# Nine-step places for a ternary quantiser inside an attention loop, its last four tiles moved to the next stage

## Chip, cores and metric

One core of a Trainium2 chip runs the whole program. The metric is device microseconds of one launch, the median of three runs. The engines are TensorE (PE, its weight loads PEld), VectorE (DVE), ScalarE (ACT), GpSimd (POOL) and the queues of DMAs issued by SyncE (SP) and ScalarE. Each takes its own instructions in order and waits on semaphores.

## What is computed

A transformer block with adaptive layer norm, B = 2, S = 1024, E = 512, 32 query heads on 8 key/value heads of 64:

```python
h = _layernorm(x) * (1 + ca) + sa
x = x + ga * attention(h, Wq, Wk, Wv, Wo)       # RoPE, causal softmax, grouped heads
h = _layernorm(x) * (1 + cb) + sb
gu = h @ ternary_quant(w_gate_up).T             # (4096, 512)
gate, up = split(gu)
hn = rms_norm(silu(gate) * up)
x = x + gb * (hn @ ternary_quant(w_proj).T)     # (512, 2048)

def ternary_quant(w, g=64):                     # in bf16, per group of 64
    scale = clip(mean(abs(w_g)), 1e-8)
    q = clip(round(w_g / scale), -1, 1)
    return w + (q * scale - w)
```

The float32 products are made of a high and a low part each (`_hi`, `_lo`), three matmuls instead of one.

## The kernel before

Four stages follow each other: a prologue (layer norm, first weights), attention, the output projection (`project_outputs`), the feed-forward network.

**Attention** runs over the 8 key/value heads g (bodies; a part of a body with g = -1 stands ahead of them and 12 steps behind them). A body is 72 steps T, written out by hand in one function `step(body, T)` per engine. Each step turns one 128 x 512 tile of exponentials (`turn`, PE L771), which ScalarE casts to `p_hi` (`high`, L855) and VectorE completes with `p_lo` (`low`, L963); two steps later TensorE multiplies it with the values (`values`, L785). So each `p_hi` and each `p_lo` marks a step. Score rows come with a period of nine steps: eight rows in nine steps, at 0, 1, 3, 4, 5, 6, 6, 7 (`ROW_AT`). A step later VectorE takes a row's maximum (`maximum`, L971, `negm`) and ScalarE its exponential (`exponentials`, L870, `p`). Score rows use four PSUM banks, so a row on TensorE waits for the exponential of two to four rows before (`ROW_FREED`). One PSUM bank collects value products; at the end of a block ScalarE copies it to `o_sb` (`copy_out`, L863), and the next block's first product waits for that.

Between these lie, at fixed steps: the projections of the next queries, keys and values on TensorE (`X_USES`), their rotation (`rotary_products`, L988 and L989, on VectorE; `rot_c`, `rot_x` on GpSimd), key casts `k_hh` (L939) and query casts `rot_s` (L943) on ScalarE, the scaling of `o_sb` on GpSimd, and the split of the next head's projection weights into high (ScalarE, T = 28) and low part (VectorE, T = 29, L1071), which TensorE's projection at T = 31 waits for.

The **quantiser** makes `ternary_quant` of one sixth of a 1/8 of the feed-forward weights at a time, six units u of 128 x 512 per body, one every 12 steps (`UNIT_STEPS`). Relative to 12u: load `wf` at 0, `w_abs` and `w_sign` on ScalarE at 3 (L947, L948), group sums `gsum` on VectorE at 4 (L1050), `gscale` at 5 (L1054), the threshold `above` at 6 (L1057), the pick (L1061) at 7, four GpSimd instructions at 8 to 11 (L1111 to L1121), store at 15 (ScalarE's queue). Units 0 to 3 are gate/up tiles, 4 and 5 down tiles; the results go to HBM. There is one place for `w_abs` and `w_sign`, so a unit's absolute values wait for the end of the unit before.

Within a step ScalarE runs, among others: `p_hi`, `o_sb`, exponentials, key and query casts, then the quantiser. VectorE: rotation, maxima, `p_lo`, then quantiser, weights' low part.

In the last body (g = 7) there is no next head to project from T = 28 on; instead the output weights and the first pieces of the attention output are split (`weights_high`, `weights_low`, `piece_high`, `piece_low`).

**The output projection** works on 4 chunks of 8 pieces; a piece is 24 matmuls and takes TensorE about 6 us. ScalarE and VectorE split the pieces of `o_raw` (L1211, L1215) with two pieces of lead. Beside it ScalarE loads stored ternary tiles (`load_tern`), TensorE turns them and ScalarE copies them for the feed-forward stage (`copy_turned`, L1328).

Of the kernel before, what the change touches and what calls it, by code (L numbers as in the profile page):

```python
# [202 lines left out]
def prologue(nc, ps, x, c, wmod, ident_in, ident, modT, hT_hi, hT_lo, vectors, late, load_first, load_tables, w_in, w_raw,  # L203
             rot, w_hi, w_lo, k_scaled, whi_ready, w_ready):
    with ExitStack() as ctx:  # L205
# [72 lines left out]
        def _(dve):  # L278
# [13 lines left out]
            dve.tensor_tensor(w_lo[:], w_raw[:], w_hi[:].bitcast(F32), ALU.subtract).then_inc(w_ready, 1)  # L292
# [48 lines left out]
UNITS, UNIT_STEPS = 6, 12  # L341
# [45 lines left out]
def attention_tensors(nc, ctx):  # L387
# [13 lines left out]
    rd_turned = sb("rd_turned", [P, 2, DEN_COLS], F32)  # L401
    wf = sb("wf", [P, UW], F32)
    w_abs = sb("w_abs", [P, UW], BF16)
    w_sign = sb("w_sign", [P, UW], BF16)
# [7 lines left out]
def attention(nc, ps, wq, wk, wv, w_gu, w_p, consts_in, w_in, w_raw, cos, sin, mask, ident, hT_hi, hT_lo, ot_dram, rden_dram,  # L412
              tern_gu, tern_p, o_sb, o_out,
              w_hi, w_lo, p_32, k_scaled, whi_ready, w_ready, vectors, late, modT, gates_dram, wmod, spare,
              tensors, rot, ident_b, tern_out, outputs):
    with ExitStack() as ctx:
# [188 lines left out]
        def _(sp):  # L605
# [42 lines left out]
            def step(body, T):  # L648
# [38 lines left out]
                if T == W_LOAD and body.holds(0, 0, KVH - 2):  # L687
                    sp.wait_ge(w_ready, body.g + 1)
# [8 lines left out]
        def _(pe):  # L697
# [139 lines left out]
        def _(act):  # L837
# [13 lines left out]

            def high(g, T):
# [29 lines left out]
            def step(body, T):  # L882
# [61 lines left out]
                for g, u in body.units(T, 3):  # L944
                    units_in.await_(act, g, u)
                    units_tern.await_(act, g, u - 1)
                    act.activation(w_abs[:], wf[:], ACT.Abs).then_inc(abs_ready, 1)  # L947
                    act.activation(w_sign[:], wf[:], ACT.Sign).then_inc(sign_ready, 1)  # L948
                for g, u in body.units(T, 15):
                    store_unit(g, u)  # L950
                for g, u in body.units(T, 0):
                    units_sign.await_(act, g, u - 1)
                    act.dma_start(unit_tile(u, wf), unit_of(g, u, gu_g, wp_g)).then_inc(wf_in, 16)

            bodies(act, step)
            outputs.scalar(act)
# [3 lines left out]
        def _(dve):  # L960
# [46 lines left out]

            def late_low(n, k):
# [4 lines left out]
            def step(body, T):  # L1013
# [34 lines left out]
                for g, u in body.units(T, 4):  # L1048
                    units_abs.await_(dve, g, u)
                    dve.tensor_reduce(gsum[:], w_abs[:].rearrange("p (g e) -> p g e", e=QG), AX.X,  # L1050
                                      ALU.add).then_inc(gsum_ready, 1)
                for g, u in body.units(T, 5):
                    units_sum.await_(dve, g, u)
                    dve.tensor_scalar(gscale[:], gsum[:], 1.0 / QG, 1e-8, ALU.mult, ALU.max).then_inc(gscale_ready, 1)  # L1054
                for g, u in body.units(T, 6):
                    units_scale.await_(dve, g, u)
                    dve.tensor_scalar(above[:], gscale[:], ROUND_HALF, None, ALU.mult).then_inc(above_ready, 1)  # L1057
                for g, u in body.units(T, 7):
                    units_above.await_(dve, g, u)
# [106 lines left out]
def project_outputs(nc, ctx, x, wo, tern_gu, tern_p, ot_dram, gates_dram, x2_dram, ident_b, wo_hi, wo_lo, places, wo_raw, wo_in, o_out,  # L1166
# [109 lines left out]
    def scalar(act):  # L1276
# [12 lines left out]
        def body(n, first):  # L1289
            if first:  # L1290
                act.wait_ge(terns_stored, 16 * UNITS * (KVH - 1))
# [550 lines left out]
```

## Time and profile before

| | |
|---|---|
| runs, median (lowest to highest) | 1844.34 us (1838.40 to 1846.98) |
| profiled execution | 1842.74 us, span 1840.8 us |
| mean granted TensorE clock | 0.992 |
| busy over the span: PE, PEld | 1745.0 us (95%), 1392.4 us (76%) |
| busy: DVE, ACT, POOL | 1260.5 (68%), 1146.8 (62%), 971.4 us (53%) |
| waits, longest in total: DVE `p_lo` for ACT `p_hi` | 187.5 us, 288 times |
| ACT `p` for DVE `negm` | 117.8 us, 153 times |
| PE scores L759 for ACT `p` | 41.6 us, 42 times |
| PE values L785 for ACT `o_sb` | 18.0 us, 31 times |

The profile is of one execution. Busy time of an engine is a share of the whole span; the stages differ, and a wait of an engine that isn't the bound costs nothing. A duration in the timeline includes time in which an instruction has been started and is held up.

### The profile page before, as it was taken

To read this page: it belongs to the slowest core of one execution; us is meant where nothing else is said; L and a number is where in the kernel's file an instruction comes from. 1 tells how busy PE (TensorE), PEld (TensorE's weight loads), DVE (VectorE), ACT (ScalarE), POOL (GpSimd) and SP (SyncE) were. 2 spreads that over 40 slices of the span, in tenths; PEclk is the share of its full clock that TensorE was granted. 3 is DMA by queue.
4 is the path that set the end of the run, shared out by engine and by line. 5 is a ranking of instruction groups with operands and counts; after the bars stand their busy time and mean duration, and the time that the engine had idled before them with its cause. 6 is when DMAs were issued, how large, how long until landed. Compare 5 with 4: busy or idle time off the path is not lost. (4 is left out here: it accounts for less than half of the span.)

```text
span 1840.8 us, 28072 instructions
## 1 busy us (share of the span) xinstructions
PE 1745.0 (95%) x9505; PEld 1392.4 (76%) x9505; DVE 1260.5 (68%) x2078; ACT 1146.8 (62%) x2315; POOL 971.4 (53%) x773
## 2 busy tenths in 40 slices
PE   7899999999999999999999999988999899999998
PEld 3587787777777777778777777866888788888886
DVE  6788888788788778788778878786333454535343
ACT  4677777777777777878777777785223353323221
POOL 1266657666667676666766666656000044444453
PEclk9999999999999999999999999999999999999999
DMA  7343444344344344344434435445555300101000
GB/s 277 88 111 84 123 106 117 102 111 127 81 127 117 85 127 113 89 118 107 124 101 108 120 89 138 110 138 170 190 183 178 130 1 1 52 1 52 1 29 23
DMA packets 174969, 190.95 MB, mean 104 GB/s; under 512 B 31456, under 2 KB 117736, under 8 KB 174832
## 3 DMA queue, kind: packets, MB, share of 16 engines
q1 hardware_dynamic: 137840, 140.99, 26.9%
q10 hardware_dynamic: 36992, 48.25, 9.4%
q8 instruction: 72, 1.18, 0.3%
q14 instruction: 65, 0.53, 0.1%
HBM read 86.12 MB, written 31.74 MB: 64 GB/s over the span
## 5 line engine op out<-in xcount | busy, mean ns | idle before, releaser
L963 DVE TENSOR_TENSOR p_lo<-ps_b,p_hi 128x512 fp32r<-128x512 f32 x576 | 395.6, 687 | 191.4 <-ACT p_hi L855 187.5
L870 ACT ACTIVATE p<-ps_b,negm 128x640 f32<-128x640 f32 (+7 forms) x512 | 382.0, 749 | 120.7 <-DVE negm L971 117.8
L855 ACT CAST p_hi<-ps_b 128x512 fp32r<-128x512 f32 x576 | 337.2, 588 | 152.8 <-PE ps_b L771 150.1
L971 DVE TENSOR_REDUCE negm<-ps_b 128x1 f32<-128x640 f32 (+7 forms) x512 | 376.1, 745 | 35.4 <-PE ps_b L761 34.7
L771 PE MATMUL ps_b<-ident,p 128*128 128x128 f32 x2304 | 351.0, 275 | 7.7 <-DVE p_lo L963 6.8
L759 PE MATMUL ps_b<-k_hh,q_hl 128*128 128x512 f32 (+3 forms) x768 | 271.2, 353 | 42.7 <-ACT p L870 41.6
L785 PE MATMUL ps_b<-p_hi,v_hl 128*128 128x512 f32 x576 | 277.2, 481 | 18.3 <-ACT o_sb L863 18.0
L771 PEld LDWEIGHTS ps_b<-ident,p 128*128 128x128 f32 x2304 | 259.1, 141 | 42.8 <-DVE p_lo L963 8.9
L760 PE MATMUL ps_b<-k_l,q_hl 128*128 128x512 f32 (+3 forms) x768 | 257.3, 348 | 0.0
L786 PE MATMUL ps_b<-p_lo,v_hl 128*128 128x512 f32 x576 | 227.9, 396 | 0.0
L759 PEld LDWEIGHTS ps_b<-k_hh,q_hl 128*128 128x128 f32 x768 | 146.0, 190 | 91.8 <-ACT p L870 60.9
L1550 PE MATMUL ps_d<-h_hi,gu 128*128 128x512 f32 x512 | 200.5, 392 | 1.9 <-DVE h_lo L1670 1.9
L1551 PE MATMUL ps_d<-h_lo,gu 128*128 128x512 f32 x512 | 199.9, 390 | 0.0
L1086 POOL TENSOR_TENSOR o_sb<-o_sb,o_low 64x512 f32<-64x512 f32 x128 | 178.5, 1399 | 37.5 <-DMA o_low<-o_sb 37.4
L1095 POOL TENSOR_TENSOR rot_c<-rot_c,rot_x 128x512 f32<-128x512 f32 (+1 forms) x96 | 126.8, 1321 | 101.6 <-DMA rot_x<-rot_s 100.8
L1106 POOL TENSOR_TENSOR rot_x<-rot_c,rot_s 128x512 fp32r<-128x512 f32 x64 | 82.2, 1284 | 165.0 <-ACT rot_s L943 165.0
L760 PEld LDWEIGHTS ps_b<-k_l,q_hl 128*128 128x128 f32 x768 | 145.7, 190 | 27.9
L1091 POOL TENSOR_TENSOR o_sb<-o_sb,rd_all 64x512 f32<-64x512 f32 x128 | 164.0, 1286 | 3.9
L723 PE MATMUL ps_b<-hT_hi,w_hi 128*128 128x512 f32 x384 | 159.3, 415 | 2.2 <-PEq L205 1.3
L1646 POOL TENSOR_TENSOR sq<-a 128x512 f32<-128x512 f32 x60 | 71.1, 1185 | 163.9 <-DVE a L1720 163.4
L724 PE MATMUL ps_b<-hT_hi,w_lo 128*128 128x512 f32 x384 | 150.8, 393 | 0.0
L725 PE MATMUL ps_b<-hT_lo,w_hi 128*128 128x512 f32 x384 | 150.3, 391 | 0.0
(159 smaller groups left out, 3202.8 us busy)
## 6 DMA issues: line engine op xcount, KB each, us to landing
rot_x<-rot_s SPq DMA_DIRECT2D x320, 64.0 KB, 2.0
q_hl<-rot_s SPq DMA_DIRECT2D x128, 128.0 KB, 2.5
q_hl<-rot_x SPq DMA_DIRECT2D x128, 128.0 KB, 2.5
rd_all<-reciprocals SPq DMA_DIRECT2D x128, 128.0 KB, 3.1
o_low<-o_sb ACTq DMA_DIRECT2D x128, 128.0 KB, 2.4
attention_out<-o_sb SPq DMA_DIRECT2D x128, 128.0 KB, 2.5
o_raw<-attention_out SPq DMA_DIRECT2D x32, 512.0 KB, 4.5
wf<-in_L_ffn_w_gate_up ACTq DMA_DIRECT2D x32, 256.0 KB, 2.9
```

The costliest lines, as they stand in the source:

```text
L759: pe.matmul(ps[:, bank, 0:n], q, k_hh[unit][:, k0:k0 + n], start=True, stop=False)
L760: ins = pe.matmul(ps[:, bank, 0:n], q, k_l0[:, unit, k0:k0 + n], start=False, stop=(k0 + n < nk))
L771: ins = pe.transpose(ps[:, T_BANK + T % 2, h * P:(h + 1) * P], p_32[:, parity, h, column * P:(column + 1) * P], ident[:])
L785: pe.matmul(ps[:, O_BANK, :], v_hl[unit][:, j, :], p_hi[:, T % P_RING, :], start=(j == 0), stop=False)
L786: pe.matmul(ps[:, O_BANK, :], v_hl[unit][:, j, :], p_lo[:, T % P_RING, :], start=False, stop=(j == i)).then_inc(pv_done, 1)
L855: act.copy(p_hi[:, T % P_RING, :], ps[:, T_BANK + T % 2, :]).then_inc(phi_ready, 1)
L870: act.activation(p_32[:, parity, h, column * P:column * P + nk], s, ACT.Exp, bias=negm[:, k:k + 1], scale=1.0, accum_out=den[:, parity, k: ...
L963: dve.tensor_tensor(p_lo[:, T % P_RING, :], ps[:, T_BANK + T % 2, :], p_hi[:, T % P_RING, :].bitcast(F32), ALU.subtract).then_inc(plo_read ...
L971: dve.tensor_reduce(negm[:, k:k + 1], s, AX.X, ALU.max, negate=True).then_inc(max_ready, 1)
L1086: pool.tensor_tensor(o_sb[0:D, n % 2, :], o_sb[0:D, n % 2, :], o_low[:, n % 2, :], ALU.add).then_inc(o_added, 1)
L1550: pe.matmul(ps[:, bank + half, :], gu[:, m, half, k, :], h_hi[:, parity, k, :], start=(k == 0), stop=False)
L1551: i = pe.matmul(ps[:, bank + half, :], gu[:, m, half, k, :], h_lo[:, parity, k, :], start=False, stop=(k == CT - 1))
```

## The change

1. The quantiser's steps go to tables with a period of nine: abs and signs at T = 8, 17, ... 53 (`UNIT_ABS`), sum, scale and threshold together at 11, 20, ... 56 (`UNIT_SUM`), pick at 17, 26, ... 62 (`UNIT_PICK`), GpSimd's parts one to four steps and the store six steps after the pick. Loads stand one step after the abs of the unit before.
2. `w_abs` and `w_sign` get two places; abs of unit u waits for the end of unit u - 2.
3. The low part of the projection weights is made in four quarters, at T = 29 to 32, and each k of the projection waits for its quarter. The prologue does it in quarters too.
4. Down tiles become units 0 and 1, gate/up tiles 2 to 5. Units 2 to 5 of the last body leave the loop: they run in the first chunk of the output projection at pieces 0, 2, 4, 6 (`LATE_UNIT_AT`), loaded into a buffer of their own (`wf_late`). The load of the last ternary tiles waits for their stores in the second chunk only.

```diff
-            dve.tensor_tensor(w_lo[:], w_raw[:], w_hi[:].bitcast(F32), ALU.subtract).then_inc(w_ready, 1)
+            for k in range(CT):
+                dve.tensor_tensor(w_lo[:, k], w_raw[:, k], w_hi[:, k].bitcast(F32), ALU.subtract).then_inc(w_ready, 1)
...
-UNITS, UNIT_STEPS = 6, 12
+UNITS = 6
+UNIT_ABS, UNIT_SUM, UNIT_PICK = (8, 17, 26, 35, 44, 53), (11, 20, 29, 38, 47, 56), (17, 26, 35, 44, 53, 62)
+UNIT_LOAD = (0,) + tuple(at + 1 for at in UNIT_ABS[:-1])
+UNIT_STORE = tuple(at + 6 for at in UNIT_PICK)
+UNIT_POOL = [tuple(at + part for at in UNIT_PICK) for part in range(1, 5)]
+LAST_UNITS = 2
...
-    w_abs = sb("w_abs", [P, UW], BF16)
-    w_sign = sb("w_sign", [P, UW], BF16)
+    w_abs = sb("w_abs", [P, 2, UW], BF16)
+    w_sign = sb("w_sign", [P, 2, UW], BF16)
...
+                        if table[u] - STEPS * back == T and self.holds(back, 0, KVH - 1 if u < LAST_UNITS else KVH - 2)]
...
-                if k == 0:
-                    if n == X_HERE:
-                        splits_lo.await_(pe, g, 0)
+                if n == X_HERE:
+                    splits_lo.await_(pe, g, k)
+                if k == 0:
...
+            def unit_raw(g, u):
+                return places.wf_late if g == KVH - 1 and u >= LAST_UNITS else wf
+            def unit_load(g, u):
+                units_sign.await_(act, g, u - 1)
+                act.dma_start(unit_tile(u, unit_raw(g, u)), unit_of(g, u, gu_g, wp_g)).then_inc(wf_in, 16)
+            def unit_parts(g, u):
+                units_in.await_(act, g, u)
+                units_tern.await_(act, g, u - 2)
+                act.activation(w_abs[:, u % 2], unit_raw(g, u)[:], ACT.Abs).then_inc(abs_ready, 1)
+                act.activation(w_sign[:, u % 2], unit_raw(g, u)[:], ACT.Sign).then_inc(sign_ready, 1)
...
-                for g, u in body.units(T, 3):
+                for g, u in body.units(T, UNIT_ABS):
+                    unit_parts(g, u)
+                for g, u in body.units(T, UNIT_STORE):
                     store_unit(g, u)
+                for g, u in body.units(T, UNIT_LOAD):
+                    unit_load(g, u)
...
+                for g, u in body.units(T, UNIT_SUM):
+                    unit_sum(g, u)
+                    unit_scale(g, u)
+                    unit_above(g, u)
+                for g, u in body.units(T, UNIT_PICK):
+                    unit_pick(g, u)
...
-                if body.split(T, W_LOW):
-                    splits_hi.await_(dve, body.g, 0)
-                    dve.tensor_tensor(w_lo[:], w_raw[:], w_hi[:].bitcast(F32), ALU.subtract).then_inc(w_ready, 1)
+                for k in range(CT):
+                    if body.split(T, W_LOW + k):
+                        splits_hi.await_(dve, body.g, 0)
+                        dve.tensor_tensor(w_lo[:, k], w_raw[:, k], w_hi[:, k].bitcast(F32), ALU.subtract).then_inc(w_ready, 1)
...
+                for part in range(4):
+                    for g, u in body.units(T, UNIT_POOL[part]):
+                        UNIT_PARTS[part](g, u)
...
+                if first and s in LATE_UNIT_AT:
+                    u = LAST_UNITS + LATE_UNIT_AT.index(s)
+                    if u > LAST_UNITS:
+                        unit_store(KVH - 1, u - 1)
+                    unit_parts(KVH - 1, u)
+                    if u + 1 < UNITS:
+                        unit_load(KVH - 1, u + 1)
...
+                if first and s in LATE_UNIT_AT:
+                    unit_scales(KVH - 1, LAST_UNITS + LATE_UNIT_AT.index(s))
...
         pool.memset(free[:], 0.0).then_inc(x2_out[1], 16)
+        for u in range(LAST_UNITS, UNITS):
+            unit_rounded(KVH - 1, u)
```

## Rows read from the trace of the kernel before

**Rows 1.** Windows: start:end, length, then busy us (instructions) per engine, PEclk, DMA share, GB/s.
```profile
531.67:681.76 150.09, 143.53 (x849) 115.30 (x848) 121.30 (x204) 115.90 (x252) 99.36 (x81) 1.00 0.42 110
1188.56:1275.50 86.94, 71.86 (x401) 54.61 (x400) 74.00 (x115) 67.67 (x139) 53.05 (x39) 0.94 0.47 139
1275.50:1333.00 57.50, 57.50 (x288) 46.79 (x287) 15.75 (x13) 15.72 (x16) 5.78 (x6) 1.00 0.65 203
```
**Rows 2.** Waits of PE in 531.67 to 681.76 us: total us, times, longest.
```profile
PE ps_b L759 <- ACT p L870: 4.2, 5, 1.3
PE ps_b L785 <- ACT o_sb L863: 2.1, 4, 0.7
```
**Rows 3.** Groups by form, attention stage: busy us, mean ns of one, idle before.
```profile
L1061 DVE TENSOR_TENSOR w_hat<-w_abs,above 128x512 bf16<-128x512 bf16 x48 | 40.8, 850 | 0.0
...
L1057 DVE TENSOR_SCALAR above<-gscale 128x8 f32<-128x8 bf16 x48 | 18.1, 378 | 0.0
```
**Rows 4.** Timeline of ACT, steps 8 and 9, and 44: start us, us, instruction, [idle before].
```profile
550.70 0.47 ACT L870 ACTIVATE p<-ps_b,negm 128x256 f32<-128x256 f32 x1 [0.60 <-DVE negm L971]
...
551.63 0.60 ACT L863 COPY o_sb<-ps_b 128x512 f32<-128x512 f32 x1
...
625.82 0.48 ACT L870 ACTIVATE p<-ps_b,negm 128x256 f32<-128x256 f32 x1 [0.37 <-DVE negm L971]
```
**Rows 5.** Timeline of DVE, a chain of dependent small instructions before the feed-forward stage.
```profile
1460.62 0.16 DVE L83 TENSOR_TENSOR tmp_d<-rstd_d 128x4 f32<-128x4 f32 x1
1460.82 0.16 DVE L84 TENSOR_TENSOR tmp_d<-tmp_d,var_d 128x4 f32<-128x4 f32 x1
```
**Rows 6.** Timeline of DVE and POOL, in the last body and in the feed-forward stage.
```profile
1196.92 1.28 POOL L1086 TENSOR_TENSOR o_sb<-o_sb,o_low 64x512 f32<-64x512 f32 x1
1197.03 1.20 DVE L1057 TENSOR_SCALAR above<-gscale 128x8 f32<-128x8 bf16 x1
...
1612.68 1.35 POOL L1648 TENSOR_TENSOR ssq<-ssq,sq 128x512 f32<-128x512 f32 x1
1612.92 1.67 DVE L1670 TENSOR_TENSOR h_lo<-h_d,h_hi 128x512 fp32r<-128x512 f32 x1
```
**Rows 7.** Timeline of DVE, step 12.
```profile
557.24 0.69 DVE L963 TENSOR_TENSOR p_lo<-ps_b,p_hi 128x512 fp32r<-128x512 f32 x1 [0.68 <-ACT p_hi L855]
```
**Rows 8.** Timeline of DVE, steps 28 to 31.
```profile
592.37 0.64 DVE L1050 TENSOR_REDUCE gsum<-w_abs 128x8 f32<-128x512 bf16 x1
...
594.66 0.40 DVE L1054 TENSOR_SCALAR gscale<-gsum 128x8 bf16<-128x8 f32 x1
594.97 1.75 DVE L1071 TENSOR_TENSOR w_lo<-w_raw,w_hi 128x1536 fp32r<-128x1536 f32 x1
596.64 0.68 DVE L963 TENSOR_TENSOR p_lo<-ps_b,p_hi 128x512 fp32r<-128x512 f32 x1
597.24 0.66 DVE L1057 TENSOR_SCALAR above<-gscale 128x8 f32<-128x8 bf16 x1
597.81 1.21 DVE L971 TENSOR_REDUCE negm<-ps_b 128x1 f32<-128x1024 f32 x1
```
**Rows 9.** Timeline of ACT and DVE, steps 39 and 40.
```profile
615.62 0.63 ACT L947 ACTIVATE w_abs<-wf 128x512 bf16<-128x512 f32 x1
...
616.28 1.07 DVE L971 TENSOR_REDUCE negm<-ps_b 128x1 f32<-128x896 f32 x1
616.80 0.58 ACT L911 COPY rot_c<-ps_b 64x512 f32<-64x512 f32 x1
...
617.89 1.01 ACT L870 ACTIVATE p<-ps_b,negm 128x896 f32<-128x896 f32 x1
```
**Rows 10.** Timeline of DVE, step 55 of the second and of the fourth body.
```profile
348.71 0.65 DVE L1061 TENSOR_TENSOR w_hat<-w_abs,above 128x512 bf16<-128x512 bf16 x1
...
648.84 1.76 DVE L1061 TENSOR_TENSOR w_hat<-w_abs,above 128x512 bf16<-128x512 bf16 x1
```
**Rows 11.** Timeline of DVE, step 67 of the last body.
```profile
1269.97 1.36 DVE L1061 TENSOR_TENSOR w_hat<-w_abs,above 128x512 bf16<-128x512 bf16 x1
```
**Rows 12.** Timeline of ACT, first piece of the output projection.
```profile
1281.27 1.05 ACT L1211 CAST o_hi<-o_raw 128x1024 fp32r<-128x1024 f32 x1 [4.96 <-PE ps_c L1260]
```

More of the change, by code:

```diff
@@ L1006, in gate_step, with unit_sum, unit_scale, unit_above @@
                                              op1=ALU.mult).then_inc(vectors.gates_done, 1)
+            def unit_sum(g, u):
+                units_abs.await_(dve, g, u)
+                dve.tensor_reduce(gsum[:], w_abs[:, u % 2].rearrange("p (g e) -> p g e", e=QG), AX.X, ALU.add).then_inc(gsum_ready, 1)
+            def unit_scale(g, u):
+                units_sum.await_(dve, g, u)
+                units_hat.await_(dve, g, u - 1)
+                dve.tensor_scalar(gscale[:], gsum[:], 1.0 / QG, 1e-8, ALU.mult, ALU.max).then_inc(gscale_ready, 1)
+            def unit_above(g, u):
+                units_scale.await_(dve, g, u)
+                dve.tensor_scalar(above[:], gscale[:], ROUND_HALF, None, ALU.mult).then_inc(above_ready, 1)
+            def unit_pick(g, u):
+                units_above.await_(dve, g, u)
+                units_out.await_(dve, g, u - 1)
+                dve.tensor_tensor(w_hat[:].rearrange("p (g e) -> p g e", e=QG), w_abs[:, u % 2].rearrange("p (g e) -> p g e", e=QG),
+                                  above[:].unsqueeze(2).broadcast_to([P, NG, QG]), ALU.is_gt).then_inc(picked, 1)
+            def unit_scales(g, u):
+                for part in (unit_sum, unit_scale, unit_above, unit_pick):
+                    part(g, u)
             def late_low(n, k):
@@ L1047, in step @@
                     dve.transpose(rd_turned[:, n % 2, :], rd[:, n % 2, :]).then_inc(rd_flipped, 1)
[L1048 to L1059, printed above, removed]
-                    units_out.await_(dve, g, u - 1)
-                    dve.tensor_tensor(w_hat[:].rearrange("p (g e) -> p g e", e=QG), w_abs[:].rearrange("p (g e) -> p g e", e=QG),
-                                      above[:].unsqueeze(2).broadcast_to([P, NG, QG]), ALU.is_gt).then_inc(picked, 1)
+                for g, u in body.units(T, UNIT_SUM):
[4 more added lines that the diff above has]
+                    unit_pick(g, u)
                 for i in range(8):
@@ L1138 @@
 TURN_LAG, COPY_LAG = 1, 2
+LATE_UNIT_AT = (0, 2, 4, 6)
 TERNS, GU_TERNS = 6, 4
@@ L1296, in body @@
                     piece_high(act, n, s, first)
+                if first and s in LATE_UNIT_AT:
[5 more added lines that the diff above has]
+                        unit_load(KVH - 1, u + 1)
+                if first and s == NPC - 1:
+                    unit_store(KVH - 1, UNITS - 1)
                 if s - COPY_LAG in TERN_AT:
@@ L1300, in body @@
                     if first and u + 2 == GU_TERNS:
+                        act.wait_ge(terns_stored, 16 * (UNITS * (KVH - 1) + LAST_UNITS))
+                    if not first and u + 2 == GU_TERNS // 2:
                         act.wait_ge(terns_stored, 16 * UNITS * KVH)
```

76 lines of the change are left out of this document (37 added, 39 removed).

## Prediction

> **What bounds the kernel now.** I read the stage windows first [rows 1]. In one steady body of the attention loop (531.67 to 681.76 us, 150.09 us for 72 steps) TensorE's matmuls are busy 143.53 us at the full granted clock, the 2.4 GHz level. So TensorE sets the time and at most 6.6 us of a body, some 46 us over seven bodies, can be won. VectorE (121.3), ScalarE (115.9) and GpSimd (99.4) all have room on average, so what counts is where their queues are late. In the stretch 1188.56 to 1275.50, the last 44 steps of the eighth body, TensorE is busy only 71.86 of 86.94 us at clock 0.94: there the other two engines set the pace. In the output projection after it TensorE is never idle. The wait view says what TensorE waits for in the body [rows 2]: score rows wait for an exponential to free a bank (4.2 us, five times), value products for the copy of `o_sb` (2.1 us, four times). Both run on ScalarE, and the exponential itself stands behind VectorE's `negm`. Each is a short in-order chain of a few steps, and the quantiser's instructions are in some of them. Steps below are T of a body; each `p_hi` cast marks one.
>
> **What one unit costs.** The change keeps every instruction of the quantiser and moves it. ScalarE pays 1.18 us from `w_abs` to the instruction behind the signs (615.62 to 616.80) [rows 9]. VectorE pays 0.6 us for `gsum`, and for `gscale`, `above` and the pick 0.07 to 0.1, 0.07 to 0.1 and 0.6 us when nothing stands in the way. They are dearer as they are: `above` averages 378 ns and the pick 850 [rows 3]. New is that sum, scale and threshold stand in one step, each waiting for the one before. Dependent small instructions follow each other every 0.20 us [rows 5], so the group costs 0.65 + 0.2 + 0.2, about 1.05 us, if GpSimd is quiet.
>
> It often isn't. `above`, eight columns wide, took 1.20 us from 1197.03, to 1198.23; GpSimd's `o_sb` had run from 1196.92 to 1198.20. And an `h_lo` that follows its own producer took 1.67 us, not 0.69, from 1612.92, because GpSimd's next instruction (1612.68) had got in between [rows 6]. So such an instruction waits for a whole GpSimd instruction of about 1.25 us, and two dependent ones can each wait. GpSimd is busy 66% of a body. A group should meet a wait of 0.66 x 0.63 = 0.4 us for the first and, if another GpSimd instruction is ready in 4 of 10 cases, 0.4 x 1.25 = 0.5 us for the second: 0.9 us on top, with ends 0 and 2.4. Worse, GpSimd's four parts now run at T=18 to 21, 27 to 30, 36 to 39, 45 to 48, 54 to 57, just where the groups of the next units stand (20, 29, 38, 47, 56).
>
> The Trainium skill says the same of the pair of ports (SBUF — State Buffer, "SBUF: two separate sides"): it is an exclusive lock that a VectorE instruction with two SBUF inputs, or in a 2-port mode, and a GpSimd instruction hold in turn, the loser blocked in full. By that rule the quarters of `w_lo` can be held up too, which the row of 1.75 us doesn't show. On the other hand the skill's VectorE: DVE Perf Modes, "The DRAIN you can't avoid", has a semaphore between chained VectorE instructions cost nothing; by it a group would be 0.8 and not 1.05 us, and the four groups of a body that matter below would cost 1.0 us less a body: 1857 us. The 0.20 us cadence speaks against it.
>
> **Place by place, per body.**
> (a) Abs and sign at T=8, ahead of `p_hi` and `o_sb` of T=9, for which TensorE's first value product waits already. ScalarE was idle for 0.60 us there, behind VectorE [rows 4], which loses scale, threshold and pick of T=5 to 7 and so ends that wait: +1.18 - 0.60 = +0.55 (0 to 1.2).
> (b) The same at T=44, behind two `k_hh` casts. The idle time before that exponential is 0.37 [rows 4], and about 0.3 comes from the sum that leaves T=40: +0.5 (0 to 1.2).
> (c) The group at T=11. VectorE had 0.68 us idle before the `p_lo` that leads to the maximum that TensorE waits for in T=14 [rows 7]. 1.05 + 0.9 - 0.68: +1.2 (0.3 to 2.5).
> (d) T=26 to 34, the worst stall now. The chain on VectorE loses `gsum` 0.56, `gscale` 0.31, the whole `w_lo` 1.67 and `above` 0.57, together 3.1 us [rows 8]. It gets the group (1.05 + 0.9) and two quarters before the maximum of T=31 (each 0.42 + 0.05, and 0.5 of blocking for both): 3.4. +0.3; the third quarter for the pick, and abs and sign one step earlier ahead of the same `w_hi`: about +0.1. +0.4 (-1.2 to 2.6).
> (e) T=39. Abs and sign leave ScalarE (-1.18), but the exponential at 617.89 can't then start before VectorE's `negm` ends at 617.35 [rows 9], and the group at T=38 adds 1.05 + 0.9 less 0.98 idle: +0.4 (-0.5 to 0.9).
> (f) T=53 to 59. The pick leaves T=55, where it took 1.76 us in five bodies of seven and 0.65 in the others, which don't stall there [rows 10]: -0.5 on average; the group at T=56 comes in: +1.0. +0.5 (-0.4 to 1.2).
> (g) Groups at T=20 and 47, in steps with more room: +0.4 (0 to 1.3). At T=62 the pick takes the place of the sum of T=64: 0.
> Sum +3.95 a body, +27.7 for seven. The eighth body has (a), (c) and half of (g): +1.9.
>
> **The four late tiles.** From T=27 of the eighth body ScalarE's four pairs (4.7 us) and VectorE's chains go; one pick alone took 1.36 us [rows 11]. On the path I count 2.3 us at T=28 to 32 (sum, blocked threshold, pick), 1.3 at 39 to 43, 1.6 at 51 to 55, 2.4 at 64 to 67, and 1.4 of GpSimd no longer blocking the weights' low parts: -9 (-5 to -12). TensorE's 15 idle us there are the ceiling; a granted clock that stays up is in it. In the output projection the same work meets ScalarE idle for 4.96 us [rows 12] and more than 5 us on VectorE per piece of 6 us. The new wait is ScalarE's for the store of the tile before, behind GpSimd's 4.6 us; queued behind it are the next `copy_turned` and `o_hi`, with about 0.7 us to spare at the third piece: +0.5 (0 to 4). Its cover is TensorE's own 6 us a piece. Prologue quarters, the second place for signs and the swapped order of tiles: 0.
>
> 27.7 + 1.9 - 9 + 0.5 = +21.1 on the profiled execution's 1842.74 us (span 1840.8), which is 1.6 below the median of the runs: **1863.8 us**.
>
> **Rivals.** (1) The gaps hold the work: GpSimd is never in the way. Then (a) and (b) 0.55 + 0.5, (c) 0.3, (d) -1.15, (e) -0.5, (f) -0.35, (g) 0: -0.65 a body, -4.6; with +0.9 in the eighth and -9: 1830 us, the other side. Its place is the group: it decides when the wait of `gscale` and `above` stays under about 0.25 us together. For it: no score row needs a maximum in steps 3, 12, 21. Against: 66% GpSimd. 0.24. (2) Gains and losses cancel: the groups are blocked but half as long, +1 a body; 7 + 1.5 - 9 + 0.5: 1843. 0.17. (3) Every group meets two full GpSimd instructions, by the skill's rule of the lock too, where GpSimd has always work ready: +7.8 a body (0.5, 0.5, 1.6, 3.3, 0.8, 1.1), 55 + 2.6 - 8 + 1: 1893. 0.14; my forecast in its own bounds 0.45.
>
> **How the numbers follow.** A measurement of this kernel tells about 0.5% (9 us) from no change. Range 1827 to 1893: from rival 1 with the last body at its -12 to rival 3. Faster 0.24 (rival 1), same 0.17 (rival 2), slower 0.59 (forecast and rival 3).
>
> **What would show it.** In the body, TensorE's wait for `o_sb` should grow at T=10 and 46 (about 0.5 us each), its wait for exponentials in T=14, 41 and 59; `above` should average over 0.6 us, the body should be 153 to 155 us long. The stretch from T=27 of the last body should fall from 86.9 to about 78 us; the output projection should stay gapless. A body of 149 us with `above` at 0.16 us would prove the forecast wrong at its main step, a longer projection at its last.

## The result and the profile after

The changed kernel took 1913.73 us (median of four runs, 1911.48 to 1919.24); beside it the kernel before took 1842.55 (1838.40 to 1846.98). The ratio is 1.0396 (95% interval 1.0381 to 1.0411): 4% slower. I had forecast 1863.8 and a range of 1827 to 1893. The direction was right, the size was not.

The page of the changed kernel, for the rows that stand in the table of before (groups: busy us, mean ns | idle time before them, and what ended most of it):

```profile
span 1909.6 us, 28143 instructions
...
PE 1771.0 (93%) x9505; PEld 1407.7 (74%) x9505; DVE 1325.5 (69%) x2102; ACT 1144.1 (60%) x2315; POOL 961.5 (50%) x773
...
L778 PE MATMUL ps_b<-ident,p 128*128 128x128 f32 x2304 | 355.2, 277 | 14.2 <-DVE p_lo L979 14.1
L766 PE MATMUL ps_b<-k_hh,q_hl 128*128 128x512 f32 (+3 forms) x768 | 273.1, 356 | 52.3 <-ACT p L890 49.8
L792 PE MATMUL ps_b<-p_hi,v_hl 128*128 128x512 f32 x576 | 280.0, 486 | 17.8 <-ACT o_sb L883 17.3
L730 PE MATMUL ps_b<-hT_hi,w_hi 128*128 128x512 f32 x384 | 165.0, 430 | 25.4 <-DVE w_lo L1102 17.9
```

And of the kernel before, for `p_lo`:

```profile
L771 PE MATMUL ps_b<-ident,p 128*128 128x128 f32 x2304 | 351.0, 275 | 7.7 <-DVE p_lo L963 6.8
```

TensorE's wait for exponentials grew from 41.6 to 49.8 us and the one for `o_sb` shrank by 0.7. What grew most is TensorE behind VectorE: from 6.8 to 14.1 us for `p_lo`, and 17.9 us for the quarters of `w_lo`, where no such wait stood before. VectorE is 65 us busier, although it has the same work: a busy VectorE instruction can be one that is held up.

**Where the 68.8 us of span went.** Windows of the kernel after (the first row is the sum of its seven full bodies, from 84.74 to 1205.17 us; then the fourth body, a stretch in it, the eighth body to its step 27 and from there on, and the output projection's first 58 us):

```profile
sum 1120.43, PE 1029.69 PEld 821.87 DVE 914.69 ACT 809.16 POOL 679.05; mean PE 147.10 PEld 117.41 DVE 130.67 ACT 115.59 POOL 97.01
...
565.57:726.41 160.84, 148.29 (x850) 118.19 (x849) 130.85 (x207) 115.47 (x252) 97.85 (x81) 0.97 0.39 103
635.80:639.00 3.20, 3.20 (x11) 2.57 (x10) 3.20 (x5) 0.87 (x1) 2.21 (x2) 0.50 0.14 48
1205.17:1262.03 56.86, 54.86 (x329) 44.67 (x328) 45.38 (x77) 42.84 (x94) 30.74 (x25) 1.00 0.40 111
1262.03:1339.40 77.37, 67.81 (x402) 51.31 (x401) 65.20 (x100) 63.34 (x131) 37.73 (x27) 0.98 0.49 141
1339.40:1397.00 57.60, 52.84 (x264) 42.31 (x263) 23.12 (x28) 19.16 (x23) 28.87 (x21) 1.00 0.66 204
```

and the sum of the seven full bodies before:

```profile
sum 1050.82, PE 1003.49 PEld 806.06 DVE 848.76 ACT 811.71 POOL 690.95; mean PE 143.36 PEld 115.15 DVE 121.25 ACT 115.96 POOL 98.71
```

The seven bodies are 69.6 us longer. TensorE's idle time in them went from 47.3 to 90.7 us (+43.4), and its busy time for the same matmuls from 1003.5 to 1029.7 (+26.2). The second part is the clock: in the fourth body the granted clock is 0.97 and not 1.00 as before [rows 1], and from 635.80 to 639.00 it is 0.50, the 1.2 GHz level. The last stretch of the eighth body fell from 86.94 us [rows 1] to 77.37, while its first 27 steps grew from 55.64 to 56.86; all of that body went from 142.6 to 134.2. Behind it everything is 4.9 us longer. Ahead of the first body it is 2.6: there TensorE is busy 66.08 us at a granted clock of 0.90, before 63.80 us at 0.96, for the same 253 matmuls. 69.6 - 8.4 + 4.9 + 2.6 = 68.7, which is the 68.8 but for rounding.

**One body, wait by wait.** TensorE's idle times in the fourth body after (timeline of PE, [idle before <- what ended it]; not shown are seven with 3.61 us together, which were there before or are small):

```profile
586.55 0.50 PE L792 MATMUL ps_b<-p_hi,v_hl 128*128 128x512 f32 x1 [0.36 <-ACT o_sb L883]
596.55 0.44 PE L766 MATMUL ps_b<-k_hh,q_hl 128*128 128x384 f32 x1 [1.26 <-ACT p L890]
...
635.45 0.58 PE L730 MATMUL ps_b<-hT_hi,w_hi 128*128 128x512 f32 x1 [2.52 <-DVE w_lo L1102]
...
666.91 0.50 PE L792 MATMUL ps_b<-p_hi,v_hl 128*128 128x512 f32 x1 [0.74 <-ACT o_sb L883]
674.92 0.50 PE L730 MATMUL ps_b<-hT_hi,w_hi 128*128 128x512 f32 x1 [0.87 <-DVE rot_s L1005]
...
695.70 0.66 PE L778 MATMUL ps_b<-ident,p 128*128 128x128 f32 x4 [1.33 <-DVE p_lo L979]
698.54 0.80 PE L766 MATMUL ps_b<-k_hh,q_hl 128*128 128x512 f32 x1 [1.72 <-ACT p L890]
```

They stand in T = 10, 14, 31, 46, 49, 58 and 59. Before, three others stood in T = 32, 41 and 59:

```profile
600.32 0.33 PE L759 MATMUL ps_b<-k_hh,q_hl 128*128 128x128 f32 x1 [0.97 <-ACT p L870]
...
619.04 0.38 PE L759 MATMUL ps_b<-k_hh,q_hl 128*128 128x256 f32 x1 [0.56 <-ACT p L870]
...
656.37 0.50 PE L759 MATMUL ps_b<-k_hh,q_hl 128*128 128x512 f32 x1 [0.60 <-ACT p L870]
```

**What stands behind T = 31 and 58.** Timeline of DVE, steps 29 and 56, and then of POOL at both places:

```profile
631.60 2.32 DVE L1035 TENSOR_SCALAR above<-gscale 128x8 f32<-128x8 bf16 x1
633.83 1.57 DVE L1102 TENSOR_TENSOR w_lo<-w_raw,w_hi 128x384 fp32r<-128x384 f32 x1
...
691.50 3.55 DVE L1035 TENSOR_SCALAR above<-gscale 128x8 f32<-128x8 bf16 x1
694.97 0.68 DVE L979 TENSOR_TENSOR p_lo<-ps_b,p_hi 128x512 fp32r<-128x512 f32 x1
```

```profile
631.50 1.16 POOL L1125 TENSOR_TENSOR w_hat<-w_abs,w_hat 128x512 bf16<-128x512 bf16 x1
632.62 1.25 POOL L1146 TENSOR_TENSOR rot_c<-rot_c,rot_x 128x512 f32<-128x512 f32 x1
...
691.39 1.16 POOL L1125 TENSOR_TENSOR w_hat<-w_abs,w_hat 128x512 bf16<-128x512 bf16 x1
692.52 1.28 POOL L1142 TENSOR_TENSOR o_sb<-o_sb,rd_all 64x512 f32<-64x512 f32 x1
693.76 1.26 POOL L1157 TENSOR_TENSOR rot_x<-rot_c,rot_s 128x512 fp32r<-128x512 f32 x1
```

`above`, 8 columns wide, was started at 691.50, 0.11 us behind a GpSimd instruction, and ended at 695.05, when `rot_x` ended: three GpSimd instructions, two of which began after it. At 631.60 it was two. The `p_lo` and the first quarter of `w_lo` stand behind it in VectorE's queue, and TensorE behind these. The same comes back in every body: `above` takes 3.55 to 3.57 us at each T = 56, and 2.3 us at T = 29 in five of seven bodies (3.42 in one; in the last of the seven the scale takes 2.42 instead). That gave my theory A: such instructions are held up by a whole run of GpSimd's, and nearly all of the loss hangs on it. The rivals: the quarters of `w_lo` do it (B), the chaining of small dependent instructions (C), or the placement of the other parts (on ScalarE, and the two places).

### The profile page after: what moved, and what is told of

Read it like the earlier page. It is cut to its first block and busy times, and to the rows that moved or that the text cites. A ratio compares the mean times of both kernels' runs of the same rounds, so it can differ in the third digit from the quotient of the medians.

```text
span 1909.6 us, 28143 instructions
## 1 busy us (share of the span) xinstructions
PE 1771.0 (93%) x9505; PEld 1407.7 (74%) x9505; DVE 1325.5 (69%) x2102; ACT 1144.1 (60%) x2315; POOL 961.5 (50%) x773
## 5 line engine op out<-in xcount | busy, mean ns | idle before, releaser
L778 PE MATMUL ps_b<-ident,p 128*128 128x128 f32 x2304 | 355.2, 277 | 14.2 <-DVE p_lo L979 14.1
L766 PE MATMUL ps_b<-k_hh,q_hl 128*128 128x512 f32 (+3 forms) x768 | 273.1, 356 | 52.3 <-ACT p L890 49.8
L1137 POOL TENSOR_TENSOR o_sb<-o_sb,o_low 64x512 f32<-64x512 f32 x128 | 168.2, 1315 | 104.1 <-DMA o_low<-o_sb 104.1
L730 PE MATMUL ps_b<-hT_hi,w_hi 128*128 128x512 f32 x384 | 165.0, 430 | 25.4 <-DVE w_lo L1102 17.9
L731 PE MATMUL ps_b<-hT_hi,w_lo 128*128 128x512 f32 x384 | 156.4, 407 | 0.0
L732 PE MATMUL ps_b<-hT_lo,w_hi 128*128 128x512 f32 x384 | 155.3, 405 | 0.0
```

Source lines behind the costliest of these rows:

```text
L766: pe.matmul(ps[:, bank, 0:n], q, k_hh[unit][:, k0:k0 + n], start=True, stop=False)
L778: ins = pe.transpose(ps[:, T_BANK + T % 2, h * P:(h + 1) * P], p_32[:, parity, h, column * P:(column + 1) * P], ident[:])
L1137: pool.tensor_tensor(o_sb[0:D, n % 2, :], o_sb[0:D, n % 2, :], o_low[:, n % 2, :], ALU.add).then_inc(o_added, 1)
```

## The experiments

All ratios are against the kernel before on the same chip.

| kernel | us | ratio, 95% interval |
|---|---|---|
| e1 old places, late tiles | 1841.43 | 1.0000 (0.9990 to 1.0011) |
| e2 whole low part | 1912.15 | 1.0390 (1.0371 to 1.0408) |
| e3 group in three steps | 1879.94 | 1.0215 (1.0195 to 1.0235) |
| e4 summing form | 1849.55 | 1.0046 (1.0029 to 1.0063) |
| e5 old places, late tiles, summing | 1833.99 | 0.9962 (0.9946 to 0.9977) |
| e6 before, summing | 1830.85 | 0.9947 (0.9932 to 0.9962) |
| e7 GpSimd's parts apart | 1878.69 | 1.0198 (1.0179 to 1.0216) |
| e8 threshold fused into the pick | 1846.05 | 1.0025 (1.0012 to 1.0038) |
| e9 = e5, late tiles untied | 1825.32 | 0.9926 (0.9912 to 0.9939) |
| e10 = e6, threshold fused | 1830.72 | 0.9951 (0.9937 to 0.9964) |
| e11 = e4, whole low part | 1845.64 | 1.0033 (1.0020 to 1.0046) |
| e12 = e9, threshold fused | 1822.90 | 0.9912 (0.9899 to 0.9926) |

TensorE's idle time in the fourth body, in us (from the timelines of PE: at two places, and in all):

| kernel | T = 31, 32 | T = 58, 59 | whole body |
|---|---|---|---|
| before | 0.97 | 0.60 | 6.6 |
| after | 2.52 | 3.05 | 12.5 |
| e2 whole low part | 3.69 | 3.08 | 13.4 |
| e3 group in three steps | 1.97 | 2.70 | 11.3 |
| e7 GpSimd's parts apart | 3.75 | 0 | 11.0 |
| e4 summing form | 3.22 | 0 | 7.8 |
| e8 threshold fused | 3.19 | 0 | 7.5 |

### e1: the places undone

```diff
-UNIT_ABS, UNIT_SUM, UNIT_PICK = (8, 17, 26, 35, 44, 53), (11, 20, 29, 38, 47, 56), (17, 26, 35, 44, 53, 62)
+UNIT_ABS, UNIT_SUM, UNIT_SCALE, UNIT_ABOVE, UNIT_PICK, UNIT_STORE = [tuple(12 * u + at for u in range(6)) for at in (3, 4, 5, 6, 7, 15)]
+UNIT_LOAD = tuple(12 * u for u in range(6))
...
-                for k in range(CT):
-                    if body.split(T, W_LOW + k):
+                if body.split(T, W_LOW):
```

> The changed kernel with the quantiser's steps of the kernel before (period of twelve, sum, scale, threshold and pick in four steps) and the whole low part in one instruction; the four late tiles, the swapped order of tiles and the two places stay. Theory: all of the loss in the bodies comes from the places. Then a body is 150.1 us again, the stretch of the last body stays at about 78.7 us (-8.2) and the later stages keep their +5: 1839 us, ratio 0.998 (0.996 to 1.000). Rival: the second places or the order of tiles cost in the bodies by themselves; then a body stays over 152 us and the ratio is over 1.005.

The body is 150.05 us again, and the last body 132.5. Windows of e1 (fourth body, eighth body, first 57 us of the output projection), and what TensorE and VectorE wait for at the start of the output projection (us in total, times, longest):

```profile
532.10:682.15 150.05, 143.44 (x849) 115.28 (x848) 120.48 (x204) 115.84 (x252) 99.51 (x81) 1.00 0.42 110
1133.18:1265.70 132.52, 122.18 (x730) 95.94 (x729) 110.07 (x176) 106.37 (x225) 70.04 (x53) 0.99 0.47 130
1265.70:1323.00 57.30, 51.98 (x254) 41.39 (x253) 22.46 (x28) 19.16 (x23) 28.94 (x21) 0.97 0.65 202
```

```profile
PE ps_c L1305 <- DVE o_lo L1262: 5.3, 3, 3.1
...
DVE w_hat L1039 <- DMA ternary<-w_hat: 8.1, 2, 5.8
```

So the order of the tiles and the second places cost nothing in the bodies, and the rest of the change alone is the loss. The four late tiles gain 10 us in the last body (142.6 to 132.5) and give back 5.9 behind it (571.2 us to the end of the span, not 565.3). In the medians nothing of it is left.

### e2 and e11: the quarters undone, with and without what stands ahead of them

```diff
-                for k in range(CT):
-                    if body.split(T, W_LOW + k):
-                        splits_hi.await_(dve, body.g, 0)
-                        dve.tensor_tensor(w_lo[:, k], w_raw[:, k], w_hi[:, k].bitcast(F32), ALU.subtract).then_inc(w_ready, 1)
+                if body.split(T, W_LOW):
+                    splits_hi.await_(dve, body.g, 0)
+                    dve.tensor_tensor(w_lo[:], w_raw[:], w_hi[:].bitcast(F32), ALU.subtract).then_inc(w_ready, CT)
```

> The changed kernel, only the low part of the projection weights made in one instruction at T = 29 again. Theory A (the threshold in T = 29 stands 2.3 us behind GpSimd's instructions, and all that is queued behind it is late): the low part still starts 2.8 us late, so the wait of the projection in T = 31 stays at 2.5 to 3.5 us and the ratio at 1.035 to 1.040. Theory B (the quarters do it: each can be held up by itself, 1.57 and 1.04 us instead of 0.5): the wait in T = 31 falls under 1 us, the body loses 3 us or more, ratio 1.025 or less.

> e4 with the whole low part in one instruction at T = 29. In e2 the quarters could show nothing, because what stood ahead of them was 2.5 us late. Here nothing is: if quarters help at all (a projection that can start after the first), this kernel loses against e4 1 us a body, ratio 1.008 to 1.010; if a quarter that waits for GpSimd costs as much as it saves, it stays at 1.0046 +- 0.002.

e2 is the changed kernel within 0.1%, and its wait at T = 31 is longer and not shorter (3.69 us, where I had said 2.5 to 3.5): the quarters are not the cause, theory B falls. e11 takes away the threshold's wait first (as e4, below), and even then the whole is not worse than the quarters (1.0033 against 1.0046, the intervals overlap), where I expected 1.008 if quarters helped. The low parts in the summing kernels e4 and e11 (count: ns min/median/max):

```profile
L1104 DVE TENSOR_TENSOR w_lo<-w_raw,w_hi x28: 540/1080/2786, 144.7 to 1060.0; 128x384 fp32r<-128x384 f32 x28
```

```profile
L1103 DVE TENSOR_TENSOR w_lo<-w_raw,w_hi x7: 3648/3906/5022, 145.1 to 1049.0; 128x1536 fp32r<-128x1536 f32 x7
```

A quarter takes 0.54 us alone and up to 2.79 held up, the whole never less than 3.65 here, against 1.75 in the kernel before [rows 8]. Both are held up themselves in the new places. That the quarters lose by four chances of being held what they win by an early start fits this, but no run shows it by itself.

### e3: the group taken apart

```diff
+UNIT_SCALE, UNIT_ABOVE = tuple(at + 1 for at in UNIT_SUM), tuple(at + 2 for at in UNIT_SUM)
...
+                for g, u in body.units(T, UNIT_SCALE):
                     unit_scale(g, u)
+                for g, u in body.units(T, UNIT_ABOVE):
                     unit_above(g, u)
```

> The changed kernel with scale and threshold one and two steps behind the sum (T = 12, 21, 30 ... and 13, 22, 31 ...), the period of nine and all else as it is. Theory A (a wait for GpSimd's run of back-to-back instructions, placed in front of the first quarter and of a p_lo cast): the first quarter in T = 29 no longer stands behind the threshold, the wait in T = 31 falls by 2 us or more, that of T = 58 to 60 by 2 us or more, since GpSimd's run is broken up differently; ratio 1.015 to 1.028. Theory C (only the small dependent instructions cost, 0.2 us each): -0.4 us a group in the four groups that matter, ratio 1.033. Rival: scale and threshold are held up just as long in their new steps and hit the projection's quarters from there: ratio 1.035 or more.

### e7: GpSimd's parts moved away from the group

```diff
-UNIT_STORE = tuple(at + 6 for at in UNIT_PICK)
-UNIT_POOL = [tuple(at + part for at in UNIT_PICK) for part in range(1, 5)]
+UNIT_STORE = tuple(at + 7 for at in UNIT_PICK)
+UNIT_POOL = [tuple(at + part for at in UNIT_PICK) for part in (1, 2, 4, 5)]
```

> The changed kernel (plain scale and threshold) with GpSimd's four parts at one, two, four and five steps behind the pick and the store at seven, so that none stands in the step of the group (three steps behind a pick). Theory A1 (it is the coincidence of the quantiser's own parts with the groups): the threshold of T = 29 and 56 falls to one GpSimd instruction or less (under 1.3 us), the waits of T = 31 and 58 to 60 lose 4 us together, ratio 1.010 to 1.022. Theory A2 (GpSimd's other work is enough: the two o_sb instructions and a rotation make the same run): the two thresholds stay over 2 us and the ratio over 1.030.

Both win half of the loss back (1.0215 and 1.0198), inside what theory A and A1 asked, but not in the way they said: in e3 the wait at T = 31 falls from 2.52 to 0.18 us, but 1.8 us come in at T = 32, and at T = 58 and 59 only 0.3 goes; in e7 the second place loses its wait whole and the first has 1.2 us more. In both an instruction of the group is still held up. Here are `above` and `gscale` of the kernel after:

```profile
L1035 DVE TENSOR_SCALAR above<-gscale x48: 171/1146/3565, 111.1 to 1375.0; 128x8 f32<-128x8 bf16 x48
...
L1031 DVE TENSOR_SCALAR gscale<-gsum x48: 170/274/2420, 109.7 to 1374.8; 128x8 bf16<-128x8 f32 x48
```

and `gscale` of e3, in its step behind the sum:

```profile
L1032 DVE TENSOR_SCALAR gscale<-gsum x48: 161/671/3256, 108.1 to 1342.7; 128x8 bf16<-128x8 f32 x48
```

In e7 the two places part ways. The wait at T = 56 is gone, as A1 said; at T = 29 it grew, as A2 said, and fell on the scale (timeline of DVE):

```profile
617.05 2.63 DVE L1031 TENSOR_SCALAR gscale<-gsum 128x8 bf16<-128x8 f32 x1
619.72 1.19 DVE L1035 TENSOR_SCALAR above<-gscale 128x8 f32<-128x8 bf16 x1
620.82 1.58 DVE L1102 TENSOR_TENSOR w_lo<-w_raw,w_hi 128x384 fp32r<-128x384 f32 x1
...
678.59 0.17 DVE L1035 TENSOR_SCALAR above<-gscale 128x8 f32<-128x8 bf16 x1
```

The GpSimd instructions ahead of the first of these lines:

```profile
616.01 1.28 POOL L1142 TENSOR_TENSOR o_sb<-o_sb,rd_all 64x512 f32<-64x512 f32 x1
617.26 1.28 POOL L1146 TENSOR_TENSOR rot_c<-rot_c,rot_x 128x512 f32<-128x512 f32 x1
```

The scale came 0.24 us before the end of `o_sb` and waited for `rot_c` and a `w_hat` behind it as well. So neither the quantiser's own parts alone nor GpSimd's other work alone make the run. Theory C (0.2 us for each dependence) asked 1.033 of e3; it falls. (The trace of e7 is of its longest execution, 1888.73 us; the median is 1878.69.)

### e4: the instructions that can't be held up

```diff
-                dve.tensor_scalar(gscale[:], gsum[:], 1.0 / QG, 1e-8, ALU.mult, ALU.max).then_inc(gscale_ready, 1)
+                dve.tensor_scalar(gscale[:], gsum[:], 1.0 / QG, 1e-8, ALU.mult, ALU.max,
+                                  accum_out=unused[:, 0:1]).then_inc(gscale_ready, 1)
...
-                dve.tensor_scalar(above[:], gscale[:], ROUND_HALF, None, ALU.mult).then_inc(above_ready, 1)
+                dve.tensor_scalar(above[:], gscale[:], ROUND_HALF, 0.0, ALU.mult, ALU.max,
+                                  accum_out=unused[:, 1:2]).then_inc(above_ready, 1)
```

> The changed kernel with scale and threshold in the form that also sums its output into a spare word (accumulator output); same places, same values. It tells whether scale and threshold are held up as instructions that take the ports shared with GpSimd, which the summing form does not do by the Trainium skill's page SBUF - State Buffer. Theory A: the threshold of T = 56 falls from 3.55 to 0.2 us and that of T = 29 from 2.3 to 0.2, the waits of T = 31 and 58 to 60 fall by about 5 us together, the clock stays up; body 153 to 155 us, ratio 1.012 to 1.022. Rival: the duration is a wait for something else (a semaphore of GpSimd's scaling of the unit before) and stays: ratio 1.04.

The threshold of e4, all 48 of it, and the windows of its fourth body:

```profile
L1036 DVE TENSOR_SCALAR_CACHE_REDUCE above<-gscale x48: 160/161/164, 106.8 to 1310.4; 128x8 f32<-128x8 bf16 x48
```

```profile
533.80:685.10 151.30, 143.48 (x849) 115.15 (x848) 122.62 (x219) 115.58 (x252) 97.91 (x81) 1.00 0.42 109
```

From 171 to 3565 ns the threshold went to 160 to 164, at the same places, against the same GpSimd work; the ratio went from 1.0396 to 1.0046. By the medians some 63 of 71 us hang on the form of two instructions of eight columns. It beat even my figure for theory A (1.012 to 1.022; a body of 153 to 155 us). Of the body's 9.5 us, 4.7 are idle time, near the 5 that I expected: the wait at T = 58 and 59 is gone, that at T = 31 fell to 1.43, but 1.8 us of waits came in at T = 32. The other 4.8 are the clock, which I had named and not counted in full: it is 1.00 and TensorE's busy time 143.48 us, as before the change. The 26 us of slow matmuls were a consequence of the waits, not a loss of their own.

The Trainium skill states the rule by which I chose this experiment (SBUF — State Buffer, "Who interferes with whom"): `tensor_scalar` can take the port pair that VectorE shares with GpSimd, but not in the form that also writes its accumulator, and `tensor_tensor` with both inputs in SBUF contends too. The rows agree on each: `above` in its two forms, and the quarters of `w_lo`, which are held up in e4 still.

### e5 and e6: the same in the old places, with and without late tiles

e6 is the kernel before with e4's two edits (an accumulator output for `gscale` and for `above`), e5 is e1 with the same two.

> The old places with the late tiles (as e1) and, besides, scale and threshold in the summing form. Theory A (such an instruction is held up by GpSimd wherever it stands, in the old places by 0.3 to 1.1 us now and then): the threshold of T = 30 falls from 0.57 to 0.17 us and the body from 150.1 to 149.3 us, ratio 0.996. Rival: in the old places nothing on the path hangs on it, the ratio stays at 1.000 +- 0.001; or the second instruction of the summing form (0.08 us) costs and it is 1.002.

> The kernel before, with scale and threshold in the summing form only. Beside e5 it tells what the four late tiles bring by themselves: their last body is 9.8 us shorter and the stages behind it 5.9 us longer in e1. If that holds, this kernel is at 0.998 and e5 0.002 below it; if the late tiles bring nothing in the runs, both are the same.

The kernel before was paying too: e6 is 0.5% faster than it. Its fourth body:

```profile
526.00:675.20 149.20, 143.18 (x849) 115.22 (x848) 118.44 (x216) 116.10 (x252) 98.79 (x81) 1.00 0.41 110
```

Against e4's 151.30 that also says what the new places, quarters included, cost when nothing is held up in scale and threshold: 2.1 us in this body, 16.3 in the seven (1056.75 against 1040.45). The late tiles I had expected to bring e5 under e6; it is 3 us above, with overlapping intervals: as built they bring nothing.

### e8 and e10: no threshold instruction

```diff
-                dve.tensor_tensor(w_hat[:].rearrange("p (g e) -> p g e", e=QG), w_abs[:, u % 2].rearrange("p (g e) -> p g e", e=QG),
-                                  above[:].unsqueeze(2).broadcast_to([P, NG, QG]), ALU.is_gt).then_inc(picked, 1)
+                dve.scalar_tensor_tensor(out=w_hat[:].rearrange("p (g e) -> p g e", e=QG),
+                                         in0=gscale[:].unsqueeze(2).broadcast_to([P, NG, QG]), scalar=ROUND_HALF,
+                                         in1=w_abs[:, u % 2].rearrange("p (g e) -> p g e", e=QG),
+                                         op0=ALU.mult, op1=ALU.is_lt).then_inc(picked, 1)
...
-                    unit_above(g, u)
```

> The changed kernel without the threshold instruction: the pick multiplies the scale by the constant itself and compares, in one instruction (scalar_tensor_tensor), and gscale keeps its plain form. Theory A: gscale takes over the wait, since it is an instruction of the same kind that is ready 0.2 us earlier; only the second wait goes (0.2 + half of 2 us): the waits of T = 31 and 58 to 60 lose 1 to 3 us, ratio 1.015 to 1.030. Rival (only the threshold is affected, not the scale): as in e4, ratio 1.005.

> The kernel before without the threshold instruction (the pick multiplies and compares in one) and with the scale in the summing form. If the single threshold instruction and its 0.2 us behind the scale are on the path anywhere in the old places, this is 0.001 to 0.002 under e6 (0.9947); else the same as e6.

e8 refuted me: the plain scale did not take over the wait, and 1.0025 is as good as e4 (the intervals overlap). The timeline of DVE in its T = 29, and of POOL:

```profile
597.36 0.27 DVE L1031 TENSOR_SCALAR gscale<-gsum 128x8 bf16<-128x8 f32 x1
597.55 2.82 DVE L1103 TENSOR_TENSOR w_lo<-w_raw,w_hi 128x384 fp32r<-128x384 f32 x1
```

```profile
596.32 1.28 POOL L1143 TENSOR_TENSOR o_sb<-o_sb,rd_all 64x512 f32<-64x512 f32 x1
597.57 1.15 POOL L1126 TENSOR_TENSOR w_hat<-w_abs,w_hat 128x512 bf16<-128x512 bf16 x1
598.69 1.25 POOL L1147 TENSOR_TENSOR rot_c<-rot_c,rot_x 128x512 f32<-128x512 f32 x1
```

The scale was started 0.24 us before `o_sb` ended and got in at the boundary, ahead of `w_hat`. The quarter behind it came as this `w_hat` began, and waited for it and for `rot_c`, as the threshold did in the kernel after. In e7 the scale was just as early against the same `o_sb`, but `rot_c` was next, and it did not get in: how early it is does not decide by itself. e10 is e6 again (0.9951 and 0.9947): in the old places no one waits for the threshold once it can't be held.

### e9 and e12: late tiles that hold nobody up

```diff
-                    if u > LAST_UNITS:
-                        unit_store(KVH - 1, u - 1)
...
-                for part in (unit_sum, unit_scale, unit_above, unit_pick):
+                for part in (unit_sum, unit_scale, unit_above):
...
+                if first and s - 1 in LATE_UNIT_AT:
+                    unit_pick(KVH - 1, LAST_UNITS + LATE_UNIT_AT.index(s - 1))
...
+                pool.dma_start(to, unit_tile(u, w_hat)).then_inc(places.late_out, 16)
```

> As e5 (old places, summing form, late tiles), but in the output projection the pick stands one piece later, behind the low part of that piece, and GpSimd issues the stores of the four tiles itself, so neither VectorE's low parts nor ScalarE's high parts stand behind a store. Theory D: the three waits of TensorE for o_lo (5.3 us in e1) are all that the late tiles cost there; they go, and the kernel is 5 to 7 us under e5: ratio 0.993. Rival: the cost is GpSimd and VectorE holding each other up, or DMA traffic: ratio 0.996 as e5.

> e9 and e10 together: old places, no threshold instruction, summing scale, late tiles with their stores on GpSimd. If the gains add up: 0.991 to 0.993; if e10 brings nothing: as e9.

In e1 the pick of a late tile waited for the store of the tile before, and the copies on ScalarE stood behind a store that waited for GpSimd (timelines of DVE and of ACT in e1; the pick, and the copy behind the last store):

```profile
1307.83 0.69 DVE L1039 TENSOR_TENSOR w_hat<-w_abs,above 128x512 bf16<-128x512 bf16 x1 [5.82 <-DMA ternary<-w_hat]
```

```profile
1314.69 1.01 ACT L1387 COPY wp_b<-ps_t 128x1024 bf16<-128x1024 bf16 x1 [8.94 <-POOL w_hat L1130]
```

The store that this pick waited for was issued at 1299.80 us, as soon as GpSimd had ended, and took 7.9 us to land (the median of these stores is 2.4); four loads of `o_raw` were issued from 1296.61 on. In e9 the longest of the four late stores takes 4.6 us, the pick waits 2.6 us in all, with no low part behind it, and TensorE has no wait for `o_lo` in the output projection's first chunk:

```profile
1257.70:1315.00 57.30, 57.30 (x287) 46.67 (x286) 23.18 (x37) 20.12 (x24) 27.44 (x25) 1.00 0.70 227
```

e9 is 6.6 us under e5 by the ratios (0.9926 and 0.9962, their intervals just apart): theory D holds, though e9 doesn't part the moved pick from the moved stores. The late tiles are a gain of their own once untied: e12 with them is at 0.9912, e10 without them at 0.9951, and the intervals are apart (those of e9 and e6, 0.9926 and 0.9947, overlap). e12, with the threshold fused as well, is 2.4 us below e9, which its interval doesn't tell from it. At 0.9912 it is 16 us faster than the kernel before and 91 us faster than the change.

## Why the prediction was wrong

The fourth body after against the one before, TensorE's idle time by place:

| place | forecast | measured |
|---|---|---|
| (a) T = 10, `o_sb` | +0.55 | +0.36 |
| (b) T = 46 | +0.5 | +0.03 |
| (c) T = 14 | +1.2 | +1.26 |
| (d) T = 29 to 34 | +0.4 (to 2.6) | +1.3: 2.52 at T = 31, less 0.97 at T = 32 and 0.25 at T = 29 |
| (e) T = 41 | +0.4 | -0.56 |
| (f) T = 58, 59 | +0.5 (to 1.2) | +2.45 |
| (g) T = 23, 24, 49 | +0.4 (to 1.3) | +1.4 |
| T = 6 and 68 | 0 | -0.2 |
| sum of idle time | +3.95 | +6.0 |
| slow clock | 0 | +4.8 (148.29 against 143.53 us busy) |

**Right.** The sign, the mechanism (the group against GpSimd), (c) nearly to the number (in e4, with scale and threshold not held up, 0.28 is left of it), (a) within its bounds, the last body (forecast -9 + 1.9 = -7.1, measured -9.6 + 1.2 = -8.4), and that the groups would meet GpSimd's parts.

**The step that failed first: the price of a held-up instruction.** I took 0.9 us a group, from the rule that one instruction waits for one of GpSimd's; [rows 6] showed 1.20 us for that. The worst that I allowed was two instructions each waiting once, 2.4. One `above` waited for three, 3.55 us, and at T = 56 it did so in every body. Over all 48 groups `gscale` took 0.49 us and `above` 1.38 on average, 0.34 together when nothing stands in the way: 1.5 us of waiting a group, not 0.9, and most of it at the two places that TensorE waits behind. In the kernel before the longest scale took 1217 ns and the longest threshold 1203, so its rows did not show this; but I had noted that GpSimd's parts would now stand exactly there, and priced the coincidence with an average of 66% busy instead of laying the two queues side by side. In T = 56 they are `o_sb`, `w_hat`, `o_sb`, `rot_x`, `w_hat` without a gap. Side by side the queues would have shown that run, and not yet that the threshold is passed over in it.

**The second: the clock.** I gave the bodies no price for it, although [rows 1] show 0.94 in the stretch with idle time and 1.00 in the full bodies. It was 26 of the 70 us, and e4 shows that it follows the waits.

**The third: two signs.** In (e) the wait went away (0.56 to none), where I had the group eat the gain of abs and sign. Why isn't shown: in e2 and e7, with the same places for them, 0.61 and 0.26 us stand there. In (b) ScalarE's gap held the work.

**The output projection** I priced at +0.5 (0 to 4) and got +4.9 (5.9 in e1). I named ScalarE's wait for the store and had missed the pick's wait for that store's DMA, 7.5 us in two waits (8.1 in e1), in front of VectorE's low parts; in e9 neither holds up TensorE. **Quarters** I counted as a gain of their own by their 0.42 us each; e2 and e11 show none.

The rivals: the third (two full GpSimd instructions a group, 1893) was closest and still 20 us short: its 55 us for the bodies cover the 43.4 us of idle time and have no clock in them. The first, 1830, in which the gaps hold the work, is what the places would give if GpSimd held nothing up. The nearest to it is e4, in which the quarters are still held up (2.79 us at most), and it is 1849.6: even then the places cost.

**What stays open.** Why an instruction is passed over once or twice and at another boundary let in. In the kernel after, 14 scales and thresholds waited for more than one GpSimd instruction, and in each of these runs one is a rotation (`rot_c` or `rot_x`). In the traces of all seven kernels that keep a plain scale or threshold (before, after, e1, e2, e3, e7, e8) there are 49 such cases, with a rotation of 128 partitions in each; and each time that such a rotation followed without a gap, the waiting instruction was passed over. Ahead of other instructions it mostly got in. That is a count, no cause, and no experiment was made on it. Of the 2.6 us ahead of the first body 2.3 are TensorE at a lower clock (above), and why it is lower there is open: the first body starts between 81.1 us (e6) and 84.9 (e7) in these kernels, and from 60 to 82 us their clocks are 0.92 and 0.79.

## What to carry to other kernels

Before a small VectorE instruction is moved in front of something that TensorE waits for, lay GpSimd's queue beside it: its price can be that of the run of GpSimd instructions that stands there, not its own 0.17 us and not one of theirs. If it must stand there, use a form that isn't held up (here the one that also sums its output, 0.16 us every time); in the kernel before this alone brought 0.5%. And a tile's work that is put off into another stage brings its store along: whoever waits for that store should have nothing urgent queued behind it.

## What the runs showed of the hardware

- A waiting VectorE instruction does not always come next in turn. The Trainium skill says (SBUF — State Buffer, "🔬 SBUF: two separate sides") that whichever instruction starts first has the shared ports for its whole length and the other is blocked. Taken as a wait for that one instruction, it would be about 1.3 us here, and the kernel before agrees (1.22 at most). The kernel after doesn't; measured there and in e8: 3.55 us (three GpSimd instructions, two of them begun after it), 2.32 (two), and 2.82 for a `tensor_tensor` of 384 columns that takes 0.54.
- It happens to the plain `tensor_scalar` of 128x8 and to `w_lo` (both inputs in SBUF). `above` as a `tensor_scalar` with an accumulator output took 160 to 164 ns in all 48 cases, and 0.08 us more for reading the accumulator.
- A wait of 2.52 us in the middle of a body at full clock was followed by 3.2 us at a granted clock of 0.50; the bodies of e4, in which no wait was over 1.43 us, ran at 1.00. Half of the 3.2 us, 1.6, is lost on top of the wait. It isn't so behind every long wait: one of 3.05 us at 1115.07 in the kernel after left the clock at 1.00 (window 1109:1122).
- The store of one tile took 7.9 us to land (e1, issued at 1299.80), while pieces of the attention output were being loaded; the median of these stores is 2.4.
